# Vision tower on one core: image tiles summed with fewer accumulating transfers, the mask inside the score product, the second variance on GpSimd

## What is computed

```python
pooled = x.reshape(64, 12, 14, 16, 14, 16).sum(axis=(3, 5))    # 16x16 patches of 12 channels
h = einsum('bcij,ce->bije', pooled, channel_weights)            # 64 x 196 tokens of 192
a = layernorm(h)
scores = q k^T / sqrt(16) + causal mask of -10000               # 12 heads
attn_out = softmax(scores) v @ out_w + out_b
sel = softmax((a @ sel_w + sel_b) / temperature)[..., 1:]
idx = top_k(sel, 14)                                            # 14 tokens of an image are chosen
y = a.at[idx].add((attn_out * sel)[idx])
h = h + y
return h + gelu(layernorm(h) @ in_w.T + in_b) @ out_w
```

## Time and profile before

| | |
|---|---|
| Median of 3 runs | 710.67 us (710.17 to 711.61) |
| The profiled execution | 711.4 us |
| Its span in the trace | 709.7 us |
| Busy: PE, DVE | 583.1 us (82%), 533.0 us (75%) |
| Busy: ACT, POOL | 342.9 us (48%), 156.6 us (22%) |

### The profile page before, as it was taken

The page is one execution under the profiler, slowest core; times in us unless marked ns, Lnnn a source line. Parts: engine busy times, 40 slices in busy tenths (PEclk is TensorE's granted clock), DMA queues, the critical chain, the costliest instruction groups (busy, mean ns, idle before and its releaser), DMA issues.

```text
span 709.7 us, 12208 instructions
## 1 busy us (share of the span) xinstructions
PE 583.1 (82%) x3860; PEld 469.5 (66%) x3860; DVE 533.0 (75%) x1357; ACT 342.9 (48%) x826; POOL 156.6 (22%) x212
## 2 busy tenths in 40 slices
PE   0237268989997998989988959989998999899995
PEld 0126146667966786768776847768776877778774
DVE  0695968798979798888978865888989897855411
ACT  0000236565656556565656435565656474647451
POOL 1021312131232223222322203222322223102001
PEclk9967557999999999999999979999999999999999
DMA  9997998999999999999999998899999997501011
GB/s 315 298 330 221 289 308 201 304 270 316 259 315 267 317 253 313 286 296 277 282 316 251 286 231 248 229 304 241 305 308 278 280 282 214 109 9 37 4 35 40
DMA packets 66382, 172.56 MB, mean 243 GB/s; under 512 B 4457, under 2 KB 56873, under 8 KB 60171
## 3 DMA queue, kind: packets, MB, share of 16 engines
q1 hardware_dynamic: 32512, 110.11, 44.3%
q0 software_dynamic: 26112, 44.73, 35.5%
q10 hardware_dynamic: 7690, 16.89, 7.1%
HBM read 158.99 MB, written 12.73 MB: 242 GB/s over the span
## 4 chain that ended last, share of the span: by engine, by line
PE 32%; DVE 27%; DMA 18%; issue 13%; ACT 5%; POOL 2%; ACTq 2%; POOLq 0%; DVEq 0%
PE psO L590 9%; DVE R L888 8%; DMA X<-in_x 6%; DMA patch_sums<-R 5%; DMA OB<-in_ob 5%; PE psS L529 3%; PE psS L541 3%; PE psF L578 2%; PE psC L565 2%; DVE a_ln L898 2%; DVE y_ln L902 2%; DVE b_ln L900 2%; ACT Sm L703 2%; PE psS L550 2%; DVE mx L1014 2%
## 5 line engine op out<-in xcount | busy, mean ns | idle before, releaser
L590 PE MATMUL psO<-W,act 128*112 128x192 f32 x1344 | 268.2, 337 | 15.3 <-issue 8.6
L888 DVE TENSOR_REDUCE R<-X 128x42 f32<-128x1344 f32 (+1 forms) x112 | 235.7, 2138 | 29.6 <-DMA X<-in_x 29.5
L590 PEld LDWEIGHTS psO<-W,act 128*112 128x112 f32 x1344 | 220.8, 182 | 22.2 <-issue 9.9
L725 ACT ACTIVATE act<-psF 128x392 f32<-128x392 f32 x192 | 95.4, 497 | 131.8 <-PE psF L578 111.9
L344 POOL DMA_DIRECT2D X<-in_x x64 | 84.3, 1442 | 51.4 <-DMA X<-in_x 45.8
L578 PE MATMUL psF<-Stk,M1S 104*128 104x392 bf16 x192 | 66.9, 348 | 9.8 <-ACT act L725 9.3
L353 POOL TENSOR_TENSOR Pt<-Praw 48x196 f32<-48x196 f32 x16 | 8.5, 534 | 225.3 <-DMA Praw<-patch_sums 208.0
L703 ACT ACTIVATE Sm<-Sm,rinv 112x196 f32<-112x196 f32 x96 | 35.2, 445 | 21.7 <-DVE rinv L1019 21.5
L578 PEld LDWEIGHTS psF<-Stk,M1S 104*128 104x128 bf16 x192 | 18.8, 98 | 39.5 <-ACT act L725 24.0
L698 ACT ACTIVATE Sm<-Sm,nm 112x196 f32<-112x196 f32 x96 | 42.6, 445 | 4.8 <-issue 4.7
L732 ACT ACTIVATE obuf<-psO 112x192 f32<-112x192 f32 x112 | 36.0, 321 | 18.3 <-PE psO L594 18.3
(11 more groups left out here) (189 smaller groups left out, 870.6 us busy)
## 6 DMA issues: line engine op xcount, KB each, us to landing
X<-in_x SPq DMA_DIRECT2D x48, 1344.0 KB, 7.7
X<-in_x SPq DMA_DIRECT2D x64, 672.0 KB, 7.5
X<-in_x POOLq DMA_DIRECT2D x64, 672.0 KB, 13.7
out<-obuf ACTq DMA_DIRECT2D x16, 588.0 KB, 7.2
patch_sums<-R ACTq DMA_DIRECT2D x16, 147.0 KB, 8.9
Praw<-patch_sums ACTq DMA_DIRECT2D x16, 147.0 KB, 6.0
W1T<-in_w1t ACTq DMA_DIRECT2D x1, 576.0 KB
W<-in_w ACTq DMA_DIRECT2D x1, 576.0 KB
```

The costliest lines, as they stand in the source:

```text
L590: pe.matmul(to, act_sb[u % 2][:, m, i * OT:(i + 1) * OT], W2[:, m, :], start=(m == 0), stop=False)
L725: act.activation(act_sb[u % 2][:, n // 2, (n % 2) * (GT // 2):(n % 2 + 1) * (GT // 2)], psF[:, 0:GT // 2], ACT.Gelu).then_inc(act_F1.sem, 1)
L888: dve.tensor_reduce(R[:, r, t * TQ * N:(t + 1) * TQ * N].rearrange("p (q j) -> p q j", q=TQ), v, AX.XY, ALU.add).then_inc(dve_L, 1)
```

## The change

- Only X3 stays a tile with an accumulating DMA. X0 and X5 are loaded whole, and a GpSimd addition (`halve`, step H) puts the second half of their rows onto the first in place; DVE reduces 1344 numbers of them. X1, X2, X4 and X6 are loaded whole and reduced whole.
- The mask leaves DVE: FM and UB get 56 more rows (64 to 119). FM's hold a one where a token comes after the query's own, UB's a diagonal of -10000, so that the product L529 brings the mask along, with 120 rows in place of 64. Sg is padded to 128 columns so that positions land on partitions 64 to 119. DVE's addition L1010 goes; the maximum and the exponentials read PSUM.
- `var2` and its root go from DVE to POOL (`second_variance`, 18 small instructions).
- All four plans are reordered; END grows by one, with the scatter at lag 5. The diff, cut to its core:

```diff
+KM = ZR + SLOTS
-ADDED = (0, 2, 4, 6)
-END = NG + 4
+ADDED = (3,)
+HALVED = (0, 5)
+END = NG + 5
...
-        FM = [sb(f"FM{i}", [ZR, T]) for i in range(2)]
+        FM = [sb(f"FM{i}", [KM, T]) for i in range(2)]
-        Sg = sb("Sg", [HALF, 2, 2, SLOTS])
+        Sg = sb("Sg", [HALF, 2, 2, ODD])
-        RM = sb("RM", [ROWS, T])
-        UB = sb("UB", [ZR, HP, 2, SLOTS])
+        UB = sb("UB", [KM, HP, 2, SLOTS])
...
+            def halve(g, t):
+                pool.wait_ge(x_in[t], loaded(g))
+                v = X[t][:, :].rearrange("p (q r w) -> p q r w", q=TQ, r=QR)
+                pool.tensor_tensor(v[:, :, 0:2, :], v[:, :, 0:2, :], v[:, :, 2:4, :], ALU.add).then_inc(x_halved[t], 1)
...
+            def rsqrt(g, steps, t):
+                by_itself(pool)
+                pool.tensor_scalar(t["h"][:, :], t["x"][:, :], -0.5, None, ALU.mult).then_inc(steps.sem, 1)
+                pool.tensor_scalar(t["y"][:, :].bitcast(i32), t["x"][:, :].bitcast(i32), -0.5, float(0x5F3759DF),
+                                   ALU.mult, ALU.add).then_inc(steps.sem, 1)
+                for k in range(3):
+                    pool.wait_ge(steps.sem, steps.at(g, f"y{k - 1}" if k else "g"))
+                    pool.tensor_tensor(t["a"][:, :], t["y"][:, :], t["y"][:, :], ALU.mult).then_inc(steps.sem, 1)
+                    pool.wait_ge(steps.sem, steps.at(g, f"a{k}"))
+                    pool.tensor_tensor(t["b"][:, :], t["a"][:, :], t["h"][:, :], ALU.mult).then_inc(steps.sem, 1)
+                    pool.wait_ge(steps.sem, steps.at(g, f"b{k}"))
+                    by_itself(pool)
+                    pool.tensor_scalar(t["b"][:, :], t["b"][:, :], 1.5, None, ALU.add).then_inc(steps.sem, 1)
+                    pool.wait_ge(steps.sem, steps.at(g, f"c{k}"))
+                    pool.tensor_tensor(t["y"][:, :], t["b"][:, :], t["y"][:, :], ALU.mult).then_inc(steps.sem, 1)
+                pool.wait_ge(steps.sem, steps.at(g, "y2"))
+            def second_variance(g):
+                pool.wait_ge(dve_R1.sem, dve_R1.at(g, "y2"))
...
+                rsqrt(g, pool_R2, n2)
...
-            plan = ("X:4:1 X:6:1 K:v:2 K:d1:2 K:d2:2 X:0:0 c:s:4 X:2:0 P:s:1").split()
+            plan = ("X:3:1 P:s:2 c:s:5 H:5:1 A:var2:2 K:v:2 K:d1:2 K:d2:2 H:0:0").split()
...
-                        mm = pe.matmul(psS[0:ROWS, 0, ZR:ZR + 1 + GB], Sg[:, k, :, :].rearrange("p d s -> p (d s)"),
+                        mm = pe.matmul(psS[0:2 * ODD, 0, ZR:ZR + 1 + GB], Sg[:, k, :, :].rearrange("p d s -> p (d s)"),
...
-            plan = ("o:0.2:2 o:1.0:2 A:zt:1 o:1.1:2 o:1.2:2 o:2.0:2 o:2.1:2 o:2.2:2 S:et:2 o:3.0:2 o:3.1:2 S:g:2 "
-                    "K:tr1:1 o:3.2:2 K:tr2:1 f:0:1 o:4.0:2 A:sl:1 o:4.1:2 at:0:2 at:1:2 at:2:2 f:1:1 o:4.2:2 f:2:1 "
-                    "A:st:1 o:5.0:2 f:3:1 G:ga:1 f:4:1 o:5.1:2 f:5:1 G:u:1 f:6:1 o:5.2:2 C:xt:2 o:6.0:2 f:7:1 C:fa:2 "
-                    "S:sc:1 f:8:1 o:6.1:2 f:9:1 o:6.2:2 f:10:1 A:tm:0 f:11:1 C:fb:2 o:0.0:1 o:0.1:1 C:f2:2").split()
+            plan = ("S:et:2 o:3.0:2 o:3.1:2 o:3.2:2 S:g:2 K:tr1:1 o:4.0:2 o:4.1:2 K:tr2:1 f:0:1 o:4.2:2 A:sl:1 "
+                    "at:0:2 at:1:2 f:1:1 o:5.0:2 f:2:1 at:2:2 f:3:1 A:st:1 o:5.1:2 f:4:1 G:ga:1 f:5:1 o:5.2:2 f:6:1 "
+                    "G:u:1 f:7:1 o:6.0:2 o:6.1:2 f:8:1 C:xt:2 o:6.2:2 C:fa:2 f:9:1 S:sc:1 f:10:1 C:fb:2 A:tm:0 "
+                    "f:11:1 C:f2:2 o:0.0:1 o:0.1:1 o:0.2:1 o:1.0:1 A:zt:0 o:1.1:1 o:1.2:1 o:2.0:1 o:2.1:1 o:2.2:1").split()
...
-                    act.activation(Sm[:, j, :], Sm[:, j, :], ACT.Exp, bias=nm[:, j:j + 1],
+                    act.activation(Sm[:, j, :], psS[0:ROWS, j // 2, (j % 2) * T:(j % 2 + 1) * T], ACT.Exp, bias=nm[:, j:j + 1],
...
-            plan = ("S:e2:2 S:e3:2 S:e4:2 S:e5:2 O:0:2 A:fm:1 S:n:2 A:e:1 O:1:2 K:H:1 S:t:2 K:M:1 K:L:1 K:k1:1 O:2:2 "
-                    "K:k2:1 R:st:0 f:0:1 O:3:2 f:1:1 f:2:1 O:4:2 f:3:1 f:4:1 R:ld:0 f:5:1 G:rs:1 f:6:1 O:5:2 C:XH:2 "
-                    "C:ga:2 f:7:1 f:8:1 f:9:1 f:10:1 O:6:2 f:11:1 C:gb:2 S:e0:1 S:e1:1").split()
+            plan = ("S:e0:2 S:e1:2 S:e2:2 S:e3:2 S:e4:2 S:e5:2 O:0:2 S:n:2 O:1:2 A:fm:1 K:H:1 S:t:2 K:M:1 O:2:2 "
+                    "K:L:1 A:e:1 O:3:2 R:st:0 K:k1:1 K:k2:1 f:0:1 f:1:1 f:2:1 f:3:1 O:4:2 R:ld:0 f:4:1 f:5:1 f:6:1 "
+                    "O:5:2 f:7:1 G:rs:1 C:XH:2 f:8:1 C:ga:2 f:9:1 f:10:1 O:6:2 C:gb:2 f:11:1").split()
...
+                dve.tensor_scalar(UB[ZR:KM, :, :, :], kc("ident")[ZR:KM, ZR:KM].unsqueeze(1).unsqueeze(1)
+                                  .broadcast_to([SLOTS, HP, 2, SLOTS]), NEG, None, ALU.mult)
...
-                dve.wait_ge((x_added if t in ADDED else x_in)[t], loaded(g))
+                if t in HALVED:
+                    dve.wait_ge(x_halved[t], g + 1)
+                else:
+                    dve.wait_ge((x_added if t in ADDED else x_in)[t], loaded(g))
...
+                v = v[:, :, :, 0:2, :] if t in HALVED else v
...
-                    dve.tensor_scalar(RM[:, :], kc("iota", ROWS), psS[0:ROWS, 0, ZR:ZR + 1], NEG, ALU.is_gt, ALU.mult).then_inc(dve_G.sem, 1)
+                    dve.tensor_scalar(FM[u % 2][ZR:KM, :], kc("iota")[ZR:KM, :], psS[ZR:KM, 0, ZR:ZR + 1], None, ALU.is_gt).then_inc(dve_G.sem, 1)
...
-                    dve.tensor_tensor(Sm[:, :, :].rearrange("p (k j) t -> p k j t", k=3),
-                                      psS[0:ROWS, :, 0:2 * T].rearrange("p k (j t) -> p k j t", j=2),
-                                      RM[:, :].unsqueeze(1).unsqueeze(1).broadcast_to([ROWS, 3, 2, T]), ALU.add).then_inc(dve_S.sem, 1)
...
-            plan = ("C:os:4 S:g:3 A:top:2 S:at:3 A:slots:2 G:ga:2 C:xh:3 L:0:0 G:u:2 L:1:0 S:sc:2 A:var:1 A:log:1 "
-                    "A:var2:1 S:ri:2 L:2:0 L:3:0 L:4:0 A:sel:1 L:5:0 L:6:0").split()
+            plan = ("C:os:4 S:g:3 A:sel:2 L:0:0 A:top:2 S:at:3 A:slots:2 G:ga:2 C:xh:3 L:1:0 G:u:2 L:2:0 S:sc:2 "
+                    "A:var:1 L:3:0 S:ri:2 L:4:0 A:log:1 L:5:0 L:6:0").split()

```

More of the change, by code:

```diff
@@ L207, in program @@
         x_added = {k: sem(f"x_halves_added{k}") for k in ADDED}
+        x_halved = {k: sem(f"x_halved{k}") for k in HALVED}
         sums_out = [sem(f"sums_stored{k}") for k in range(2)]
@@ L216, in program @@
         pe_A = Steps(sem("pe_tokens"), "tm zt sl st")
-        dve_A = Steps(sem("dve_tokens"), "cp pr var ve z lr L D1 D0 t1 t2 s2 v2 den rden sel m8a mr1 m8b fx mr2 mk cs sr S S2")
+        dve_A = Steps(sem("dve_tokens"), "cp pr var ve z lr L D1 D0 den rden sel m8a mr1 m8b fx mr2 mk cs sr S S2")
         act_A = Steps(sem("act_tokens"), "fm e")
         newton = "h g " + " ".join(f"{n}{k}" for k in range(3) for n in "aby")
-        dve_R1, dve_R2, dve_RC = (Steps(sem(f"dve_rsqrt_{k}"), newton) for k in ("ln1", "ln2", "lnC"))
-        pool_K = Steps(sem("pool_stacks"), "by1 mean w d1 d2")
+        dve_R1, dve_RC = (Steps(sem(f"dve_rsqrt_{k}"), newton) for k in ("ln1", "lnC"))
+        pool_R2 = Steps(sem("pool_rsqrt_ln2"), "h g " + " ".join(f"{n}{k}" for k in range(3) for n in "abcy"))
+        pool_K = Steps(sem("pool_stacks"), "t1 t2 s2 v2 by1 mean w d1 d2")
         act_K = Steps(sem("act_stacks"), "H M L k1 k2")
@@ L230, in program @@
         pe_S = Steps(sem("pe_attention"), "sc et g at")
-        dve_S = Steps(sem("dve_attention"), "sm mx nm ri g0 g1 h1")
+        dve_S = Steps(sem("dve_attention"), "mx nm ri g0 g1 h1")
         act_S = Steps(sem("act_attention"), "e0 e1 e2 e3 e4 e5 n0 n1 n2 n3 n4 n5 t0 t1 t2")
@@ L368, in store_chosen @@
                                         ).then_inc(scat[e], 16)
+            def rsqrt(g, steps, t):
[16 more added lines that the diff above has]
+                pool.wait_ge(dve_R1.sem, dve_R1.at(g, "y2"))
+                if exists(g - 1):
+                    pool.wait_ge(pool_K.sem, pool_K.at(g - 1, "w"))
+                by_itself(pool)
+                pool.tensor_scalar(sc["t1"][:, :], n1["y"][:, :], 1.0, None, ALU.add).then_inc(pool_K.sem, 1)
+                pool.wait_ge(pool_K.sem, pool_K.at(g, "t1"))
+                pool.tensor_tensor(sc["t2"][:, :], sc["t1"][:, :], sc["t1"][:, :], ALU.mult).then_inc(pool_K.sem, 1)
+                pool.wait_ge(pool_K.sem, pool_K.at(g, "t2"))
+                pool.tensor_tensor(sc["s2"][:, :], sc["t2"][:, :], sc["var"][:, :], ALU.mult).then_inc(pool_K.sem, 1)
+                pool.wait_ge(pool_K.sem, pool_K.at(g, "s2"))
+                by_itself(pool)
+                pool.tensor_scalar(n2["x"][:, :], sc["s2"][:, :], EPS, None, ALU.add).then_inc(pool_K.sem, 1)
+                pool.wait_ge(pool_K.sem, pool_K.at(g, "v2"))
+                rsqrt(g, pool_R2, n2)
             def stage_K(g, u, part):
@@ L373, in stage_K @@
                 if part == "v":
-                    pool.wait_ge(dve_R2.sem, dve_R2.at(g, "y2"))
+                    pool.wait_ge(pool_R2.sem, pool_R2.at(g, "y2"))
                     pool.tensor_tensor(v[:, 1, :, :, 0:C], p, by_c(sc["t1"][:, :]), ALU.mult).then_inc(pool_K.sem, 1)
@@ L395, in body @@
                         add_halves(g, int(step))
```

(18 more changed lines are left out.)

9 lines of the change are left out of this document (6 added, 3 removed).

## The result

The kernel after takes 703.63 us (median of 4 runs, 700.80 to 706.07), the kernel before beside it 711.14 us (4 runs, 710.17 to 713.91): a ratio of 0.988 (0.985 to 0.992), faster by 7.5 us or 1.2%. The forecast was 687. The direction was right, the gain under a third of the 24 us forecast; the range, 670 to 716, holds the time. The profiled execution took 706.07 us with a span of 704.4; before, 711.4 and 709.7.

A forecast was written before the change was run, and what follows sets the result against it. Bound: a loop through DMA and DVE, afterwards through POOL's second root: 34.2 us + 2.35 (halving) - 1.7 (transfers) + 0.6 (PE overlap) = 35.5 a group; 711.4 - 14 x 1.7, median 0.7 lower: 687 us, range 670 to 716.

The forecast's parts named there:

- But a longer branch now decides: ACT's `R:st` waits through `K:L` for POOL's stack and second root: loop 34.2 us, 34.9 after two corrections.
- the loop before: Store of the sums, reload, POOL's addition, DVE's root and work to the next store: 37.3 us, the beat before.
- the interval with the pause: One 46.3 us interval between DVE's copies, with a 4.50 us PE pause that nothing in the profile releases; left as is.
- Both ready about when DVE arrives: `sel`, waiting for `e`, and L0, waiting for H0, are ready 12 us after the root; costed at nothing.
- GpSimd's root: POOL's second variance and root, 17 steps of 0.36 us plus 0.5: 6.6 us (bounds 3.4 and 9.3).
- rival 3: Slower by GpSimd's chain: POOL steps of 0.51 us, root 9.3 us; 739 us, or 716 with faster transfers; chance 0.20.
- The halving: Each POOL halving takes 2.85 us and blocks DVE's operations on two SBUF tiles: +2.35 us a group (bounds 0 and 3.6).
- The transfers: Store and reload of the sums shrink as three tile halves leave the software queue: -1.7 us (bounds 0 and -4).
- Rival 2: Store and reload keep their 15.8 us, hidden behind other queues' traffic anyway; loop 36.6 us, 702 us in all; chance 0.20.
- DVE's sum: DVE's work a group goes from 31.6 to 29.1 us (+1.4 tiles, -1.4 mask, -2.5 `var2`); no bound by itself.
- Rival 1: The engines' floor: PE's 34.3 us a group decides, 670 us in all; chance 0.18.
- Start and tail: Start under the weights' loads (bounds -5 to +5 us), tail under a busy PE (0 to +4); both costed at nothing.

The follow-up runs named there:

- f1: The kernel after, with one Newton round in place of three in GpSimd's second root: 691.25 us, 0.969 of before.
- a5: The kernel after, with `t` ahead of `H` on ACT and X5 added by DMA in place of the halving: 692.76 us, 0.974 of before.
- e2: a5 with X0 also added by DMA, so that GpSimd halves nothing: 679.91 us, 0.955 of before.
- e3: e2 with the first loads of X4 to X6 held back until the attention weights have landed: 672.32 us, 0.942 of before.
- b3: The kernel before, with only the tiles' part (X3 added by DMA, X0 and X5 halved by GpSimd, four whole): 774.65 us, 1.087 of before.
- b1: The kernel before, with only the mask moved into the score product: 706.91 us, 0.991 of before.
- b2: The kernel before, with only the second variance and its root on GpSimd: 709.28 us, 0.992 of before.
- d1: The kernel after, with the first loads of X4 to X6 held back until the attention weights have landed: 700.50 us, 0.982 of before.

## Why the prediction came out as it did

- **What bounds it after: wrong, and this is the step that failed.** "But a longer branch now decides" was half right: the branch through the second root does decide. But it was closed through `R:st`, the two transfers and P, 34.9 us in all, while P is ready 5.0 to 6.0 us early in most groups. With the terms as measured that loop takes 32.4 us: 10.75 from root to store (12.6 forecast), 15.8 to POOL's start (14.1 forecast), 5.8 to the next root. The chain that closes runs root, `v`, `H`, `t`, `g`, G, and then DVE's own order: 36.7. The forecast had counted `t` only within the 4.5 us from `H` to `L`, and did not ask who waits for `t`. Both plans have `K:H` ahead of `S:t`; with the longer root it now holds `t` up. f1 shows that what stands behind the second root carries time; it does not tell its branches apart (`t` and G, `e` and `sel`, H0 and L0), and `t` moved alone gained nothing. Even the loop before was tight only in every second group: there `P` ended 0.7 to 1.4 us ahead of the copy, in the others 2.0 or more, and the forecast had read one of the tight ones.
- **What the miss is made of.** The span fell by 5.3 us where 23.8 was forecast. The beat lacks 16, the start costs 5.0 and the tail 0.8, and the interval with the pause gives 3.3 back. That last part is luck.
- **"Both ready about when DVE arrives": the sentence costed at nothing.** H0 was ready 13.3 us behind the root (313.72 against 300.43), not 12, and L0 began at 13.8. In a5 L0 followed H0 by half a microsecond; e2 and e3, without H0, have the shortest beats, but against a5 that is some 0.3 us in an ordinary group and one long interval.
- **GpSimd's root: 6.6 forecast, 5.8 measured.** 18 instructions, mostly 0.20 or 0.23 us each, 0.28 to 0.42 from start to start, 0.33 on average. The bounds held, and rival 3 (a step over 0.39 us) is out. f1 prices it: 2.6 us of it give about 1 us a group.
- **The halving: 2.85 forecast, 3.03 measured** (32 of them, 3.027 on average). The lock is there, but 1.2 us a group, not 2.35, and 0.5 more on `den` under H0: H5 falls on `nm`, just ahead of the copy, in half of the groups, and in the others H5 lies under a tile's reduction, which shows no lengthening. The Trainium skill says the same (SBUF — State Buffer, "Who interferes with whom"): beside operations with two SBUF inputs it names `tensor_scalar` as one that can be locked out, where its operands meet the conditions of a 2-port mode, and `tensor_reduce` as one that never is. The forecast had looked at the first kind alone; the trace agrees on both, 2.69 us for `nm` and 2.93 for whole tiles, as elsewhere.
- **The transfers: -1.7 forecast, nothing measured.** From the store's issue at 311.18 over the reload's at 319.56 to POOL's start at 326.98 it is 15.8 us, as before, with the DMA share down from 1.03 to 0.86; over the steady groups 15.3 on average, before 14.9. Rival 2 had this right, and its 702 is the nearest of all figures, but by another mechanism: the loop that it prices has slack, and what is left is the chain through G. b3 and e3 say the same from both sides: b3, with the same tiles as the kernel after and a reload of 2.6 us, is slow, and e3, with 34.5 us of DMA a group in place of 31.5, is fast. Why the reload lands so much sooner in b3 was not looked into.
- **DVE's sum: right.** Busy 133.78 / 160 x 36.65 = 30.6 us a group, 1.2 of them the lock, against 29.1. It is no bound by itself, and b1 and b2 gain little.
- **Rival 1** needed PE without a gap; PE is busy 147 of 160, as before. e3, at 672.32, came near its 670 with the chain loosened, and a start of 74.8.
- **Start and tail: costed at 0,** with bounds of +5 and +4; measured +5.0 and +0.8. "Whole tiles compete with the weights' queue" was the reason given for the upper bound. d1 brings 4.6 us back by letting the weights go first, but OB itself came only 2.0 us later than before, and the same order of loads was not tried on the kernel before: that the cause is the whole tiles is likely, not shown.
- **Open.** The interval with the pause shrank from 46.3 to 43.0 us without an experiment on it; it is 38.9 to 46.3 us in the other kernels. PE's new wait for DVE's F (24.2 us in 9 waits) wasn't tested, nor H5 ahead of P. The chain explains where the beat stands, while the gain of 0.56 us is a difference of two bounds and isn't split further. What bounds the longer intervals of e2 and e3 (35.5 to 36.0 us; in one of 35.8 PE is busy 33.86) stays open.
